# Computing eight experts for all rows, or each for the rows routed to it

## The chip, the cores and the metric

One core of a Trainium2 chip runs the whole program in one launch. The metric is the device time of that core in microseconds, the median of several executions.

## The reference

The input is (16, 512, 192). Two layers run one after the other, each an attention block and a feed-forward block on residuals, after a first block that pools tokens to (16, 128, 192). The block that the change touches is the mixture of experts of the first layer. Rows h2 are the 16 x 128 = 2,048 normalized rows of 192 values:

```python
logits = h2 @ gate_w + gate_b
wts, sel = jax.lax.top_k(logits, TOPK)          # TOPK = 2 of E = 8
wts = jax.nn.softmax(wts.astype(jnp.float32), axis=-1).astype(x.dtype)
cw = (jax.nn.one_hot(sel, E, dtype=x.dtype) * wts[..., None]).sum(axis=1)
res = jnp.zeros_like(h2)
for e in range(E):
    he = jax.nn.gelu(h2 @ w1[e] + b1[e], approximate=False)   # 192 -> 768
    res = res + cw[:, e:e + 1] * (he @ w2[e] + b2[e])         # 768 -> 192
```

Each row has a weight other than zero for two experts only.

## The kernel before

Five engines run instruction lists of their own, written out by hand, with semaphores between them. The order of the stages is: token pooling with attention (`tok_...`, a loop over pairs of batches), two attention stages over 32 units in one schedule (`f_...`, lines 797 to 950 on TensorE), the gate and the experts, an attention with a Sinkhorn iteration (`a_...`, `t_...`), and a quantized feed-forward (`q_...`).

The gate: after `rstd_all("n3")` VectorE normalizes the rows (line 1597), TensorE turns them (line 629), ScalarE writes them out as `feat32` (line 643), and TensorE makes the logits (line 930). VectorE takes the two largest logits with their indices (lines 1601 to 1614) and makes the dense weights `cw`, rows by 8 experts (to line 1630). TensorE turns `cw` (line 938) and multiplies it by the b2 rows (line 943), and VectorE adds that to the residual `hs` (line 1650).

The experts: every product is made of bfloat16 halves, high x high + low x high + high x low. For each of 8 experts and each of 4 groups of 512 rows, `moe_up` (line 657) makes six blocks of 128 hidden values, each of 6 matmuls with 512 columns into one PSUM bank; the weights are the stationary side. ScalarE puts Gelu over each block twice, as bfloat16 (line 1309) and as float32 (line 1312), VectorE subtracts to get the low half (line 1676), and `moe_down` (line 669) multiplies four tiles of 128 rows by 18 matmuls with 192 columns; here the hidden values are the stationary side. VectorE adds each tile, scaled by its column of `cw`, to `hs` (line 1664). All 2,048 rows go through all 8 experts: 128 passes of 128 rows. On TensorE the down blocks of a group stand behind the up blocks of the next. Six experts run in a loop of three turns, two are written out. SyncE loads the weights of two experts ahead (lines 509 to 521), and ScalarE and VectorE split them between groups. GpSimd is idle from line 593 until `moe_done` (line 1686), then clears buffers for the next stage.

## Time and profile before

| | |
|---|---|
| median of 3 executions | 1895.9 us (1895.38 to 1904.0) |
| the profiled execution | 1898.1 us, its span 1896.4 us |
| mean granted TensorE clock | 0.762 of full |
| TensorE busy | 1584.9 us (84%) |
| VectorE busy | 989.3 us (52%) |
| ScalarE busy | 662.5 us (35%) |
| GpSimd busy | 115.6 us (6%) |
| DMA | 25.66 MB, 14 GB/s over the span |

The stages in the span: token stage to about 480 us, attention units to 800, gate to 855, experts to 1302, Sinkhorn attention to about 1765, quantized block to the end. Busy shares are averages over all of them; what a change in one stage is worth is read from that stage. The granted clock is given as a share of 2.4 GHz; it stands at either 1.0 or 0.5 (1.2 GHz) at any moment.

### The profile page before, as it was taken

How to read it: one execution, taken by the hardware profiler on the slowest of the kernel's cores; microseconds unless marked ns; L12 is line 12 of the kernel's file. 1: busy time of each engine (PE TensorE's matmuls, PEld its weight loads, DVE VectorE, ACT ScalarE, POOL GpSimd, SP SyncE). 2: the span in 40 equal slices, each digit the busy share in tenths (PEclk: the TensorE clock that was granted, in tenths of full speed). 3: DMA queues.
4: the chain of work that ended last, by engine and by line, in shares of the span. 5: the costliest groups of instructions: out<-in, count | busy, mean ns of one | idle time of the engine just before them, and what ended most of it. 6: DMA issues, size and time to landing. Idle time of an engine off the chain costs nothing.

```text
span 1896.4 us, 47049 instructions
## 1 busy us (share of the span) xinstructions
PE 1584.9 (84%) x20979; PEld 1301.8 (69%) x20979; DVE 989.3 (52%) x2415; ACT 662.5 (35%) x1116; POOL 115.6 (6%) x90
## 2 busy tenths in 40 slices
PE   6888888888799999879999999997578999996342
PEld 5877778777577777665766676676478898985222
DVE  4445454455356544344444444445446666665777
ACT  1122121222344433137566556653322332213130
POOL 2000000000000000000000000001234222200000
PEclk8767877778799979559999999999655555555566
DMA  4000000020000000000000000000000000000001
GB/s 155 11 7 17 17 17 10 7 66 0 1 2 2 2 2 2 1 25 26 26 16 12 26 26 1 1 1 1 1 3 4 3 4 3 3 3 2 1 1 33
DMA packets 6380, 25.66 MB, mean 14 GB/s; under 512 B 576, under 2 KB 2624, under 8 KB 5952
## 3 DMA queue, kind: packets, MB, share of 16 engines
q1 hardware_dynamic: 6208, 23.05, 3.9%
q8 instruction: 147, 2.41, 0.5%
q14 instruction: 25, 0.20, 0.0%
HBM read 21.47 MB, written 1.57 MB: 12 GB/s over the span
## 4 chain that ended last, share of the span: by engine, by line
PE 68%; DVE 18%; POOL 6%; ACT 6%; issue 2%; POOLq 0%; ACTq 0%; DVEq 0%
PE ps L657 13%; PE ps L669 10%; PE ps L703 6%; PE ps L1031 6%; PE ps L769 4%; PE ps L813 3%; DVE big L430 3%; DVE big L435 3%; POOL big L604 3%; POOL big L608 2%; PE ps L723 2%; PE ps L1079 2%; PE ps L448 2%; PE ps L875 2%; PE ps L838 2%
## 5 line engine op out<-in xcount | busy, mean ns | idle before, releaser
L657 PE MATMUL ps<-big 96*128 96x512 bf16 x1152 | 254.7, 381 | 7.5 <-issue 5.1
L1031 PE MATMUL ps<-big 128*128 128x2 bf16 x7680 | 222.4, 165 | 43.8 <-POOL big L608 20.8
L1031 PEld LDWEIGHTS ps<-big 128*128 128x128 bf16 x7680 | 215.0, 104 | 56.4 <-DVE big L1735 23.8
L1676 DVE TENSOR_TENSOR big<-big 128x512 bf16<-128x512 f32 x192 | 133.0, 693 | 148.9 <-ACT big L1312 148.9
L657 PEld LDWEIGHTS ps<-big 96*128 96x128 bf16 x1152 | 112.6, 98 | 140.4 <-issue 8.3
L669 PEld LDWEIGHTS ps<-big 128*128 128x128 bf16 x2304 | 190.9, 98 | 5.7
L669 PE MATMUL ps<-big 128*128 128x192 bf16 x2304 | 194.1, 246 | 0.0
L1309 ACT ACTIVATE big<-ps,b1cur 128x512 bf16<-128x512 f32 x192 | 131.9, 687 | 161.1 <-PE ps L657 156.1
L448 PE MATMUL ps<-ident,big 128*128 128x128 f32 x384 | 82.6, 397 | 69.3 <-ACT big L442 69.3
L1312 ACT ACTIVATE big<-ps,b1cur 128x512 f32<-128x512 f32 x192 | 130.4, 679 | 0.0
L448 PEld LDWEIGHTS ps<-ident,big 128*128 128x128 f32 x384 | 70.7, 209 | 86.0 <-ACT big L442 86.0
L703 PE MATMUL ps<-consts,big 96*128 96x192 f32 x512 | 114.6, 391 | 12.1 <-POOL iota L593 12.1
L703 PEld LDWEIGHTS ps<-consts,big 96*128 96x128 f32 x512 | 110.8, 260 | 13.0 <-issue 12.0
L1723 DVE TENSOR_REDUCE big<-ps 128x24 f32<-128x48 f32 x160 | 33.0, 206 | 142.2 <-PE ps L1031 141.6
L1664 DVE SCALAR_TENSOR_TENSOR hs<-ps,cwcur,hs 128x192 f32<-128x192 f32 x128 | 51.4, 414 | 81.6 <-PE ps L669 81.6
L442 ACT ACTIVATE big<-big 128x1536 f32<-128x1536 f32 x32 | 47.4, 1483 | 125.2 <-DVE big L435 125.2
L1351 ACT ACTIVATE big<-ps,neg_reg 128x1536 bf16<-128x1536 f32 (+1 forms) x32 | 47.5, 1537 | 108.6 <-PE ps L1016 108.6
L597 POOL MEMSET big<- 128x6144 f32 x1 | 5.2, 5222 | 1290.3 <-DVE small L1686 1290.3
L1541 DVE TENSOR_REDUCE big<-ps 128x12 bf16<-128x1536 f32 x32 | 56.3, 1758 | 50.9 <-PE ps L838 50.9
L1253 ACT ACTIVATE big<-ps 128x512 f32<-128x512 f32 x96 | 50.4, 598 | 89.9 <-PE ps L860 89.9
L430 DVE TENSOR_REDUCE big<-ps 128x3 f32<-128x768 f32 x64 | 58.2, 950 | 43.0 <-PE ps L753 43.0
L769 PEld LDWEIGHTS ps<-big 128*64 128x64 f32 x1536 | 67.8, 185 | 4.3 <-issue 4.3
(314 smaller groups left out, 2440.8 us busy)
## 6 DMA issues: line engine op xcount, KB each, us to landing
big<-w_dram SPq DMA_DIRECT2D x16, 576.0 KB, 5.3
big<-x_dram SPq DMA_DIRECT2D x16, 384.0 KB, 3.4
consts<-packed_dram SPq DMA_DIRECT2D x1, 4459.0 KB, 17.7
out_dram<-hs SPq DMA_DIRECT2D x2, 768.0 KB, 7.0
consts<-packed_dram SPq DMA_DIRECT2D x1, 1152.0 KB, 5.8
```

The source lines that it names most:

```text
L430: last = nc.vector.tensor_reduce(b.mx[:, k * g:(k + 1) * g], sc[:, k], X, ALU.max)
L435: last = nc.vector.tensor_tensor(p4[:, k], sc[:, k], b.mx[:, k * g:(k + 1) * g].unsqueeze(2).to_broadcast([P, g, keys]), ALU.subtract)
L448: last = nc.tensor.transpose(ps[s][:, k // 4, (k % 4) * P:(k % 4 + 1) * P], bufs[s].p[:, k * P:(k + 1) * P], ident[:, :])
L604: nc.gpsimd.affine_select(out=blocks, in_=blocks, compare_op=ALU.not_equal, fill=0.0, base=0, pattern=[[0, HEADS], [-1, P]], channel_multi ...
L657: last = nc.tensor.matmul(ps[0][:, q % 4, :], w1_parts[k][w][:, c, m * P:(m + 1) * P], x[:, c, g * TG:(g + 1) * TG], start=(c == 0 and w = ...
L669: last = nc.tensor.matmul(ps[1][:, t, 0:C], h[g % 2][:, m, t * P:(t + 1) * P], w2_parts[k][w][:, m, :], start=(m == 0 and w == 0 and h is ...
L703: last = nc.tensor.matmul(o[:, t, 0:C], xT[:, c, cols], tok_w[:, c, part * C:(part + 1) * C], start=(c == 0), stop=(c == 1))
L769: last = nc.tensor.matmul(ps[s][w * WQ:(w + 1) * WQ, 3, at:at + HD + 1], pT[:, l, k, w * WQ:(w + 1) * WQ], b.v_ext[:, (2 * w + k) * HEADS ...
L1031: last = nc.tensor.matmul(sums[:, 2 * k:2 * k + 2], kernel_part(i, part)[:, at:at + P], x_parts[g % 4][:, k, 0:2], start=(part == 0), stop ...
L1309: nc.scalar.activation(he_hi[g % 2][:, m, :], ps[0][:, (at - 1) % 4, :], ACT.Gelu, bias=bias)
L1312: nc.scalar.activation(he[:, m, :], ps[0][:, (at - 1) % 4, :], ACT.Gelu, bias=bias).then_inc(sem("moe_gelu"), 1)
L1676: nc.vector.tensor_tensor(he_lo[g % 2][:, m, :], he[:, m, :], he_hi[g % 2][:, m, :], ALU.subtract).then_inc(sem("moe_he_lo"), 1)
```

## The change

The experts are computed on routed rows only. The diff:

- GpSimd prepares counting masks at the start, and SyncE clears a buffer of 39 x 128 rows in DRAM (`xs`). 39 is 4,096 row places in tiles of 128, plus 7 for experts whose last tile isn't full.
- Five experts' weights (7 down to 3) are loaded during the attention stage and split to bfloat16 halves by GpSimd; three (2, 1, 0) by ScalarE and VectorE around the gate. All eight then stay in SBUF (`e_all`). The b1 values become two rows of the contraction, through a small DRAM buffer, so that a hidden block is 5 matmuls.
- TensorE turns `feat32` back to rows (`turn_back`), ScalarE and VectorE split them into a row of 384 bfloat16 values. VectorE and two matmuls count, for each row and choice, its place among its expert's rows, and the expert of each tile (`tile_e`).
- GpSimd sends each row to its two places: 32 indirect DMAs of 128 rows into `xs`. SyncE loads tile after tile, four ahead.
- For each of 39 tiles TensorE reads the expert's number into a register (`value_load`), turns the rows of tile i+2 (`m_turn`, 3 transposes), makes the hidden values of tile i+1 (`m_up`, 30 matmuls with 128 columns; the weights' address comes from the register) and the outputs of tile i (`m_down`, 6 matmuls with 384 columns and 6 with 192). ScalarE makes Gelu twice on 512 and on 256 columns, VectorE copies the rows, subtracts, and sums the two halves of the output. SyncE stores each tile's result to DRAM (`ys`).
- GpSimd fetches the results back by 32 indirect DMAs, and VectorE adds each, scaled by the row's weight, to `hs`. Then `moe_done`.

The core of it:

```diff
-        def moe_up(pe, e, k, g):
-            for m in range(HT):
-                q = g * HT + m
-
-                pe.wait_ge(sem("moe_gelu"), e * (NG * HT) + k * NG * HT + q + 1)
-
-                for c in range(2):
-                    for w, x in ((0, feat_hi), (0, feat_lo), (1, feat_hi)):
-                        last = nc.tensor.matmul(ps[0][:, q % 4, :], w1_parts[k][w][:, c, m * P:(m + 1) * P],
...
+            def m_turn(i):
+                pe.wait_ge(sem(f"m_row{i % 4}"), 16 * (i // 4 + 1))
+                if i >= 2:
+                    pe.wait_ge(sem("m_x"), i - 1)
+                o = ps[1][:, i % 2, 0:ROW // 2].bitcast(BF16)
+                for c in range(3):
+                    last = nc.tensor.transpose(o[:, c * P:(c + 1) * P], e_row[i % 4][:, c * P:(c + 1) * P], identb[:, :])
+                last.then_inc(sem("m_turned"), 1)
+
+            def m_up(i, expert):
+                pe.wait_ge(sem("m_x"), i + 1)
+                if i >= 2:
+                    pe.wait_ge(sem("m_gelu"), 2 * (i - 1))
+                x = e_x[i % 2]
+                sides = (x[:, 0:P], x[:, P:2 * P], x[:, 2 * P:3 * P], x[:, 0:P], e_xe[i % 2])
+                for m in range(HT):
+                    for k, side in enumerate(sides):
+                        at = k * HIDDEN + m * P
+                        w = e_all[:, bass.ds(expert, 1), at:at + P].rearrange("p o n -> p (o n)")
+                        last = nc.tensor.matmul(ps[0][:, 2 * (i % 2) + m // 4, m % 4 * P:(m % 4 + 1) * P], w, side,
+                                                start=(k == 0), stop=(k == CHUNKS - 1))
+                    if m in (3, 5):
+                        last.then_inc(sem("m_up"), 1)
+
+            def m_down(i, expert):
+                if i >= 2:
+                    pe.wait_ge(sem("m_y"), i - 1)
+                o = ps[1][:, 2 + i % 2, 0:2 * C]
+                for m in range(HT):
+                    if m in (0, 4):
+                        pe.wait_ge(sem("m_lo"), 2 * i + 1 + m // 4)
+                    at = CHUNKS * HIDDEN + m * 2 * C
+                    cols = slice(m * P, (m + 1) * P)
+                    for part, n in ((e_hi, 2 * C), (e_lo, C)):
+                        w = e_all[:, bass.ds(expert, 1), at:at + n].rearrange("p o n -> p (o n)")
+                        last = nc.tensor.matmul(o[:, 0:n], part[i % 2][:, cols], w, start=(m == 0 and part is e_hi),
+                                                stop=(m == HT - 1), skip_group_check=True)
+                last.then_inc(sem("m_down"), 1)
...
+            expert = older = None
+            for i in range(-1, TILES):
+                older = expert
+                if i + 1 < TILES:
+                    expert = pe.value_load(tile_e[0:1, i + 1:i + 2], min_val=0, max_val=EXPERTS - 1)
+                if 0 <= i and i + 2 < TILES:
+                    m_turn(i + 2)
+                if i + 1 < TILES:
+                    m_up(i + 1, expert)
+                if 0 <= i:
+                    m_down(i, older)
```

On SyncE (the weight loads and the tiles' rows) and on GpSimd (the split, the sending and the fetching):

```diff
+            sp.wait_ge(sem("m_zero"), 1)
+            sp.dma_start(xs.rearrange("(i p) n -> p i n", p=P),
+                         zero_row.unsqueeze(1).to_broadcast([P, TILES, ROW])).then_inc(sem("m_cleared"), 16)
...
+            sp.wait_ge(sem("m_sent"), 16 * 2 * B)
+            for i in range(4):
+                load_rows(i)
+            for i in range(TILES):
+                sp.wait_ge(sem("m_y"), i + 1)
+                sp.dma_start(ys[i * P:(i + 1) * P, :], e_y[i % 4]).then_inc(sem(f"m_stored{i % 4}"), 16)
+                if i + 4 < TILES:
+                    load_rows(i + 4)
...
+            for n, e in enumerate(EARLY):
+                split_expert(n, e)
+            pool.wait_ge(sem("f_out"), U)
+            for e in LATE:
+                nc.gpsimd.memset(e_up(e, 4), 0.0).then_inc(sem("w_zeros"), 1)
+
+            pool.wait_ge(sem("m_places"), 1)
+            for t in range(B):
+                if t % 2 == 0:
+                    pool.wait_ge(sem("m_rows"), t // 2 + 1)
+                for k in range(2):
+                    nc.gpsimd.indirect_dma_start(
+                        out=xs, out_offset=bass.IndirectOffsetOnAxis(ap=place_i[:, k, t:t + 1], axis=0),
+                        in_=row_parts[:, t, :], in_offset=None).then_inc(sem("m_sent"), 16)
+            for k in range(4):
+                pool.wait_ge(sem(f"m_stored{k}"), 16 * stores(k))
+            for j in range(2 * B):
+                if j >= 8:
+                    pool.wait_ge(sem(f"m_taken{j % 8}"), 16 * (j // 8))
+                nc.gpsimd.indirect_dma_start(
+                    out=taken[j], out_offset=None, in_=ys,
+                    in_offset=bass.IndirectOffsetOnAxis(ap=place_i[:, j % 2, j // 2:j // 2 + 1], axis=0)).then_inc(
+                        sem(f"m_taken{j % 8}"), 16)
```

## Rows read from the trace of the kernel before

**Rows 1.** The page's busy times and its 40 slices, whole span.
```profile
PE 1584.9 (84%) x20979; PEld 1301.8 (69%) x20979; DVE 989.3 (52%) x2415; ACT 662.5 (35%) x1116; POOL 115.6 (6%) x90
...
PEclk8767877778799979559999999999655555555566
```
**Rows 2.** Busy time by stretch: us, each engine, granted clock, DMA share, GB/s.
```profile
500.00:600.00 100.00, 93.22 (x1342) 68.81 (x1341) 51.08 (x136) 41.18 (x88) 0.00 (x0) 1.00 0.01 2
...
660.00:670.00 10.00, 8.52 (x129) 6.71 (x130) 6.88 (x19) 4.48 (x11) 0.00 (x0) 1.00 0.01 2
...
770.00:780.00 10.00, 9.71 (x118) 8.12 (x115) 3.06 (x7) 2.11 (x5) 0.00 (x0) 0.50 0.01 2
...
855.00:1302.00 447.00, 441.36 (x3456) 303.14 (x3456) 204.32 (x342) 268.19 (x412) 0.00 (x0) 1.00 0.05 14
```
**Rows 3.** Instruction groups, 855 to 1302: busy us, mean ns, idle before, releaser.
```profile
L1676 DVE TENSOR_TENSOR big<-big 128x512 bf16<-128x512 f32 x192 | 133.0, 693 | 148.9 <-ACT big L1312 148.9
L1309 ACT ACTIVATE big<-ps,b1cur 128x512 bf16<-128x512 f32 x192 | 131.9, 687 | 161.1 <-PE ps L657 156.1
...
L1664 DVE SCALAR_TENSOR_TENSOR hs<-ps,cwcur,hs 128x192 f32<-128x192 f32 x128 | 51.4, 414 | 81.6 <-PE ps L669 81.6
```
**Rows 4.** The chain that ended last, in order: start us, us, what.
```profile
872.95 5.94 PE ps L669 x72
878.89 7.77 PE ps L657 x36
...
1398.21 14.35 PE ps L1031 x528
```
**Rows 5.** Timeline of the gate and of the end of the experts.
```profile
807.08 5.87 PE L629 MATMUL ps<-ident,big 128*96 128x128 f32 x32 [4.89 <-DVE big L1597]
...
829.48 0.29 DVE L1601 TENSOR_TENSOR logits<-ps,consts 128x128 f32<-128x128 f32 x1 [18.10 <-PE ps L930]
...
833.33 0.18 DVE L1614 CAST gidx<-idx 128x32 f32<-128x32 uint32 x1
...
1302.18 0.06 DVE L1686 MEMSET small<- 128x1 f32 x1
```
**Rows 6.** Instruction groups, whole span: a VectorE copy of 384 columns from PSUM.
```profile
L1452 DVE COPY big<-ps 128x384 f32<-128x384 f32 x16 | 8.9, 558 | 12.5 <-PE ps L736 12.5
```
**Rows 7.** DMAs of lines 504, 521: SyncE's issue in ns; KB and landing in us.
```profile
L504 SPq DMA_DIRECT2D big<-x_dram x14: 317/317/328, 28.8 to 388.7; - x14
...
L521 SPq DMA_DIRECT2D out_dram<-hs x2: 657/674/692, 1887.0 to 1887.8; - x2
...
big<-x_dram SPq DMA_DIRECT2D x16, 384.0 KB, 3.4
```
**Rows 8.** Line 666 on TensorE's sequencer: ns minimum, median, maximum.
```profile
L666 PEldq ALU_OP  x93: 32/32/32, 872.8 to 1188.8; - x93
```
**Rows 9.** Timeline and chain of the first stage: the third load, its first use.
```profile
28.84 2.92 SPq L504 DMA_DIRECT2D big<-x_dram  x2
...
71.28 9.37 PE ps L703 x32
```
**Rows 10.** Timeline of GpSimd, 1504 to 1515 us.
```profile
1504.54 3.29 POOL L608 TENSOR_TENSOR big<-big 128x1536 bf16<-128x1536 f32 x1
...
1511.06 3.10 POOL L608 TENSOR_TENSOR big<-big 128x1536 bf16<-128x1536 f32 x1
```
**Rows 11.** Line 1786 on VectorE, beside GpSimd: ns minimum, median, maximum.
```profile
L1786 DVE TENSOR_TENSOR hs<-hs,big x8: 558/975/1393, 1503.5 to 1764.9; 128x384 f32<-128x384 f32 x8
```
**Rows 12.** The chain from 738 to 790: score blocks of successive units.
```profile
745.84 1.10 PE ps L838 x24
753.49 1.13 PE ps L838 x24
...
772.65 2.05 PE ps L838 x24
782.82 2.05 PE ps L838 x24
```

More of the change, by code:

```diff
@@ new lines, in build, with lists, temp @@
+        lists_at = XQ_AT + 2 * HIDDEN
+        def lists(at, words):
+            return big[:, lists_at + at:lists_at + at + words]
+        below = lists(0, P // 2).bitcast(BF16)
+        ones_b = lists(64, P // 2).bitcast(BF16)
+        ranks = [lists(128 + 96 * k, 96).bitcast(BF16) for k in range(3)]
+        iota_tiles = lists(416, TILES)
+        def temp(at, words):
+            return consts[:, 1920 + at:1920 + at + words]
+        chosen = temp(0, 256).rearrange("p (k b e) -> p k b e", k=2, b=B)
@@ new lines, in _, with row_lo @@
+            nc.vector.tensor_tensor(shifted(ranks[2], 0), shifted(ranks[1], 0), shifted(ranks[1], 64),
+                                    ALU.add).then_inc(sem("m_ranks"), 1)
+            def row_lo(j):
+                dve.wait_ge(sem("m_rows_hi"), j + 1)
+                nc.vector.tensor_tensor(row_parts[:, 2 * j:2 * j + 2, C:ROW], turned_back(j),
+                                        row_parts[:, 2 * j:2 * j + 2, 0:C], ALU.subtract).then_inc(sem("m_rows"), 1)
+            for k in range(4):
+                ins = nc.vector.memset(tile_sums[k], 0.0)
@@ new lines, in _, with sums @@
+            link(ins)
+            for j in range(4):
+                row_lo(j)
+            def sums(k, by=0):
+                return tile_sums[k][:, 4 - by:12 - by]
+            dve.wait_ge(sem("m_ranked"), 1)
+            link(nc.vector.tensor_scalar(sums(0), ps[0][:, 0, 2 * P:2 * P + EXPERTS], 1.0 / P, 0.494, ALU.mult, ALU.add))
+            link(nc.vector.tensor_scalar(sums(0), sums(0), ROUND, ROUND, ALU.add, ALU.subtract))
+            for k in range(3):
+                link(nc.vector.tensor_tensor(sums(k + 1), sums(k), sums(k, 1 << k), ALU.add))
@@ new lines, in _ @@
+            nc.vector.tensor_copy(place_i, place_f).then_inc(sem("m_places"), 1)
+            for j in range(4, 8):
+                row_lo(j)
+            link(nc.vector.tensor_tensor(upto, sums(3).unsqueeze(1).to_broadcast([P, TILES, EXPERTS]),
+                                         iota_tiles.unsqueeze(2).to_broadcast([P, TILES, EXPERTS]), ALU.is_le))
+            link(nc.vector.tensor_reduce(tile_f, upto, X, ALU.add))
+            link(nc.vector.tensor_scalar(tile_f, tile_f, float(EXPERTS - 1), None, ALU.min))
@@ L1683, in _, with m_x @@
-            experts(dve, expert)
-            dve.wait_ge(sem("moe_added"), EXPERTS * B + 4)
+            for k in range(2):
+                nc.vector.memset(e_xe[k][64:P, :], 1.0)
+            late_lo(1)
+            late_lo(2)
+            def m_x(i):
+                dve.wait_ge(sem("m_turned"), i + 1)
+                if i >= 2:
+                    dve.wait_ge(sem("m_up"), 2 * (i - 1))
+                rows = ps[1][:, i % 2, 0:ROW // 2].bitcast(BF16)
+                nc.vector.tensor_copy(e_x[i % 2], rows)
+                nc.vector.tensor_copy(e_xe[i % 2][0:64, :], rows[0:64, P:2 * P]).then_inc(sem("m_x"), 1)
@@ new lines, in _ @@
+            m_x(0)
+            m_x(1)
+            for i in range(-1, TILES):
+                if 0 <= i and i + 2 < TILES:
+                    m_x(i + 2)
+                if 0 < i:
+                    m_y(i - 1)
+                if i + 1 < TILES:
+                    m_lo(i + 1)
+            m_y(TILES - 1)
+            for t in range(B):
+                for k in range(2):
+                    j = 2 * t + k
+                    dve.wait_ge(sem(f"m_taken{j % 8}"), 16 * (j // 8 + 1))
+                    nc.vector.scalar_tensor_tensor(out=hs[:, t, :], in0=taken[j], scalar=gw[:, t, 2 - k:3 - k],
+                                                   in1=hs[:, t, :], op0=ALU.mult, op1=ALU.add).then_inc(sem("m_added"), 1)
+                    dve.wait_ge(sem("m_added"), j + 1)
```

342 lines of the change are left out of this document (215 added, 127 removed).

## The prediction

> **What bounds the kernel now.** I read first the page's busy times and its 40 slices [rows 1], then the engines' busy time by stage [rows 2], then the costliest groups of instructions and the chain of work that ended last, for the expert stage alone [rows 3, 4]. From 855 to 1302 us TensorE is busy 441 of 447 us at a granted clock of 1.00; VectorE is busy 204 and ScalarE 268 [rows 2]. In the chain an up block of 36 matmuls (512 columns each) takes 7.77 us, 215.8 ns apiece, and a down block of 72 (192 columns each) takes 5.94 us, 82.5 ns apiece [rows 4]. Those are 512 and 192 columns at 2.4 GHz plus 2.5 ns: the stage runs at the pace of streamed columns. For one expert and 128 rows this is 36 x 215.8 / 4 + 18 x 82.5 = 3.43 us, and 8 x 16 of them make 439 us, which is the stage. So only fewer columns help, and the change takes a large part of them away: 39 passes of 128 rows in the place of 128. The question is what the routing adds in front of and behind them, where TensorE now has no such wait.
>
> **What goes.** The old path is from the logits, which VectorE takes at 829.48 us, to the small write that releases the next stage, which ends at 1302.24 [rows 5]: 472.8 us.
>
> **What comes, in order of the path.**
>
> *Places.* From the logits to the cast of the indices takes 833.33 + 0.18 - 829.48 = 4.0 us [rows 5], plus nothing new for the gap, which only moves ahead. Behind it stand some 25 small linked VectorE instructions (ranks, tile sums, places) at 0.2 to 0.45 us, about 6 us, and four subtractions of 384 columns out of PSUM at 0.56 each [rows 6]. TensorE's turned-back rows (28 transposes before the rank matmuls) go at the 5.87 us per 32 of the stage before [rows 5] and lie beside it. I take 12.3 us in all.
>
> *Scatter.* 32 indirect DMAs on GpSimd, one behind the other on its queue. The trace has no such instruction. Bounds: SyncE issues a plain DMA of 128 partitions in 0.32 us, and one of 1,024 pieces of 768 bytes in 0.67 us; a plain DMA lands 3.4 us after its issue [rows 7]. A queue is unlikely to beat the first or, as eight may be under way in the gathers, to need the last for each. Software that reads 128 indices and writes 128 addresses is nearest to the 0.67 us of the many-piece row, and slower: I take 1.3 us, twice it. 32 x 1.3 = 41.6 us. The Trainium skill ("DMA: Bandwidth & Descriptors", Latency and other measured facts) gives about 1 us to the first byte of a DMA issued from GpSimd; no row here shows it, and by it, as an estimate, scatter and gather together would take 64 us in the place of 83, and the forecast would be 19 us lower. Under the scatter lie the three late experts' splits (ScalarE about 4.5 us and VectorE about 4 us each), the last of them with a DMA of 5 us or so, the bias rows and the b2 product; should the scatter take under 30 us, these would come forward as the bound and give back up to 10 us.
>
> *Into the loop.* Last landing 3.4, first row tile loaded 3.4 [rows 7], turn and copy 1.4: 8.2 us.
>
> *39 tiles.* TensorE's columns per tile: 30 up matmuls of 128 (55.8 ns each by the 2.5 ns rule above) 1.67 us, 3 turns 0.17, down 6 x (162.5 + 82.5) = 1.47: 3.31 us. That is the lower bound, 129 us. The weight loads don't add to it if they hide as in the old down block, and in the later stage a load and a matmul of two columns go in 14.35 / 528 = 27.2 ns [rows 4], well under 55.8. New is the sequencer's share: each weight address is made in a register. An ALU_OP on TensorE's sequencer takes 32 ns [rows 8]; 30 for the up loads and about 6 for the down ones are 1.15 us, the 90 loads and matmuls at 13.6 ns each are 1.22, five lone waits perhaps 0.25: 2.6 us, under 3.31 and therefore hidden if it can run ahead. Not in the trace is the load of the expert's number into the register, once per tile. Bounds: 0 (hidden behind the queued down matmuls) and 3.4 us (as a DMA's landing), that is a tile of 3.3 to 6.0 us. Small, a read of one word by the sequencer, it is nearer to the lower; I take 1.4 us, a sequencer-bound tile of 4.0 us, 156 us in all. ScalarE needs two activations of 512 at 0.69 and two of 256 at about 0.45, 2.3 us; VectorE 0.56 (x) + 0.25 + 0.69 + 0.43 (low parts) + 0.56 (sum out of PSUM), 2.5 us, with waits 2.8 [rows 3, 6]: neither is the bound. SyncE issues two DMAs a tile (0.7 us) four tiles ahead of need. First tile at the lower clock and the last tile's chain through ScalarE and VectorE: 6 us.
>
> *Here a rule of the skill speaks against the change.* The row shows 192-column pairs at 82.5 ns, loads fully hidden [rows 4]. The Trainium skill ("TensorE: Matmul & The Clock Gate", Back-to-back issue gap) says that streams of load and matmul at 128 columns sustain about 81 ns per matmul, not 56. Were that so, the up part of a tile would be 2.43 us and the tile's columns 4.07, an estimate; it is the first half of rival A below.
>
> *Back.* Last sum and store 4, 32 gathers at 1.3 = 41.6, last landing 3.4 and two additions at 0.42 [rows 3] with their links 0.9: 49.9 us. The additions run behind the gathers, shorter than these.
>
> Sum: 12.3 + 41.6 + 8.2 + 156 + 6 + 49.9 = 274.0 us against 472.8: 198.8 less.
>
> **What is moved elsewhere.** (a) Clearing the row buffer: a store of 3.8 MB is put on SyncE's queue at about 12 us, ahead of the third and fourth input loads. They are issued at 28.8 and first used at 71.3 [rows 9]; even 25 us of store leave 20 us over. If that cover were gone, it would cost what the loads are late, once. (b) Five experts' weights are split on GpSimd during the attention stage, which has no GpSimd work now. A GpSimd subtraction of 1,536 columns takes 3.10 us, and 3.29 beside heavier VectorE work; a VectorE addition of 384 columns that meets it takes 0.56 us at best and 1.39 at worst [rows 10, 11]. So the two disturb each other. GpSimd would need about 12 us per expert, done by about 600 us with loads, long before use. VectorE is busy 51 us in the first 100 us of that stage [rows 2]; 6% of it is 3 us, and one blocked instruction of 0.8 us (384 GpSimd columns) in each of 13 units would be 10. TensorE's chain hides a part; I take 4. (c) The loop's branches and the old memsets go with the old stage, in the 472.8 already. (d) Behind the stage nothing is changed; TensorE arrives cold, but already before it waited 9 us there.
>
> Net: -198.8 + 4 = -194.8. The profiled execution took 1898.1 us (span 1896.4), so 1703 us; the median is 2.2 lower, within the error of all this.
>
> **Rivals.**
> *A. The tile loop is slow* (tile of 5.5 to 6.4 us). Either weight loads, addresses and the register read come one after the other with the matmuls, or TensorE stays at the lower clock: twice 3.2 is 6.4 us. For it: each tile has a sequencer-only instruction between blocks. Against: at 85% busy the attention stage held 1.00 [rows 2]. 39 x (6.4 - 4.0) = +94: 1797 us.
> *B. An indirect DMA takes 2.8 us* on GpSimd: 64 x 1.5 = +96, 1799 us. For it: software per row. Against: nothing in the trace.
> *C. The attention stage loses the clock.* A unit there takes 7.65 us at 1.00 (745.84 to 753.49) and 10.17 at 0.50 (772.65 to 782.82) [rows 2, 12]; it fell by itself late in the stage. If the GpSimd work makes it fall early, up to 24 units x 2.5 us = +61: 1764 us.
> *D. Slower than before.* The indirect DMAs cost over (194.8 / 64) + 1.3 = 4.3 us each, for instance because each waits for its 128 single-row writes in turn (the plain landing of 3.4 us plus 1 us of software). At 5 us the time is 1703 + 64 x 3.7 = 1940 us. It decides from 4.3 us.
> That the change doesn't do what it says is hardly open: 39 tiles are fixed in the code, full or not.
>
> **How the numbers follow.** Forecast 0.62, A 0.14, B 0.14, C 0.06, D 0.04 (of which a quarter within 0.5%). 0.5% is about what a measurement here can tell from no change. The forecast's own lower end has the DMA at 0.67 us (-40) and the tile at 3.3 to 3.6 (-16 to -27): about 1640; its upper end, with 1.8 us and 4.6 us, 1758. To hold 8 in 10 the range takes in most of A and B: 1630 to 1800. Faster 0.95, same 0.01, slower 0.04.
>
> **What would show it.** Right: TensorE idle for about 45 us from 843 us and again for about 48 us before the next stage; between them some 39 equal periods of 4.0 us with the clock at 1.00; GpSimd's queue full in both gaps; the attention stage within 5 us of before. Wrong: periods over 5 us, or at 0.50 (A); gaps over 80 us (B, D); more 0.50 slices before 800 us (C); the first tile waiting for the late weights or bias rows and not for the scatter.

## The result and the profile after

The changed kernel takes 1785.4 us (median of 4 runs, 1782.7 to 1788.4), the kernel before, on the same chip, 1897.0 (4 runs): 0.9405 of it, with an interval of 0.9377 to 0.9434. That is 112 us less; forecast were 195 less, and 1630 to 1800 us as the range. So the direction and the range held, and the forecast's centre was 82 us too low. The profiled execution took 1785.9 us (span 1784.1).

The page of the kernel after, its busy times and the granted clock in 40 slices of 44.6 us (rows 1 of before answer to them):

```profile
PE 1401.8 (79%) x19314; PEld 1182.7 (66%) x19314; DVE 901.0 (51%) x2335; ACT 472.0 (26%) x878; POOL 239.4 (13%) x248
...
PEclk9777786877687978685569999858555555555566
```

TensorE has 183 us less to do. From the twelfth slice on, the attention stage has only one slice at nine tenths, where it had four before [rows 1]. The same as numbers, busy time by stretch (us, each engine, granted clock, DMA share, GB/s); the first three lie in the attention stage, then come the scatter, the loop over the 39 tiles, and the gathers:

```profile
500.00:600.00 100.00, 92.81 (x1130) 67.56 (x1129) 51.86 (x102) 36.22 (x78) 54.40 (x85) 0.86 0.29 86
600.00:700.00 100.00, 92.97 (x1262) 70.21 (x1259) 56.71 (x172) 39.38 (x87) 0.61 (x1) 0.88 0.07 20
700.00:800.00 100.00, 97.15 (x1270) 74.78 (x1268) 40.50 (x91) 33.06 (x74) 0.00 (x0) 0.76 0.01 2
871.00:914.00 43.00, 12.93 (x48) 11.01 (x48) 17.68 (x29) 10.50 (x11) 33.81 (x31) 0.54 0.35 112
918.00:1144.00 226.00, 223.12 (x1755) 160.30 (x1755) 80.30 (x195) 68.00 (x156) 0.00 (x0) 0.98 0.12 35
1147.00:1186.00 39.00, 0.00 (x0) 0.00 (x0) 12.23 (x30) 0.00 (x0) 29.55 (x32) 0.52 0.27 76
```

The marks between the parts, from the timelines of VectorE, GpSimd and TensorE (start us, us, what; in brackets the idle time before and what ended it):

```profile
860.10 0.29 DVE L1781 TENSOR_TENSOR logits<-ps,consts 128x128 f32<-128x128 f32 x1 [17.20 <-PE ps L1042]
...
871.04 1.21 POOL L727 DMA_INDIRECT rows_dram<-consts  x1 [35.01 <-DVE consts L1838]
...
920.14 0.54 PE L1100 MATMUL ps<-big 128*128 128x128 bf16 x3 [0.48 <-DVE big L1891]
...
1143.77 0.56 DVE L1905 TENSOR_REDUCE big<-ps 128x192 f32<-128x384 f32 x1 [0.91 <-PE ps L1116]
1146.82 0.99 POOL L735 DMA_INDIRECT big<-results_dram,consts  x1 [231.50 <-DMA results_dram<-big]
...
1188.92 0.06 DVE L1926 MEMSET small<- 128x1 f32 x1
```

So the logits come 860.10 - 829.48 = 30.6 us later than before [rows 5], although nothing ahead of them was to change but GpSimd's work, the loads of the weights and the clearing of the row buffer. Of these 30.6 us 2.6 lie ahead of the attention stage (its first normalisation starts at 496.76 in the place of 494.19), 28.0 in it. From there the new path takes 1188.98 - 860.10 = 328.9 us, where the old one took 472.8. What follows took 594.2 us before and takes 595.1 now. 30.6 - 143.9 + 0.9 = -112.4, the difference of the spans. Two terms are larger than forecast: the tile loop, and the attention stage.

The loop. The chain of work that ended last, one tile of it, after the same for two more (start us, us, what):

```profile
985.93 1.64 PE ps L1116 x12
987.58 0.17 PE ps L1087 x3
987.74 3.94 PE ps L1100 x30
...
991.68 1.64 PE ps L1116 x12
```

A tile takes 991.68 - 985.93 = 5.75 us at a clock of 1.00. The down block (L1116) takes 1.64 and the turn (L1087) 0.17, near the 1.47 and 0.17 forecast. The up block of 30 matmuls (L1100) takes 3.94, where its columns need 1.67. What TensorE's queue and its sequencer (PEldq) did there, in ns (minimum, median, maximum), and six weight loads in the timeline:

```profile
L1100 PEldq FUSED_REGOPS  x1170: 46/46/65, 920.0 to 1140.3; - x195
L1100 PEld LDWEIGHTS ps<-big x1170: 95/96/105, 920.1 to 1140.4; 128*128 x195
...
L1131 PEldq TENSOR_LOAD <-consts x39: 297/302/491, 919.2 to 1135.8; - x39
...
L1116 PEldq FUSED_REGOPS  x234: 46/46/46, 928.5 to 1142.2; - x117
...
987.92 0.71 PEld L1100 LDWEIGHTS ps<-big 128*128 x6
```

Six loads span 0.71 us and the last lasts 0.096, so they start (0.71 - 0.096) / 5 = 0.123 us apart. Each has a register operation of 46 ns ahead of it, which makes its address. The down block has only 6 of these for its 12 matmuls and longer matmuls to lie behind.

The attention stage. VectorE's normalisation of 192 columns in it (first row before, second row after; SBUF to SBUF), in ns:

```profile
L1531 DVE TENSOR_SCALAR big<-hs,meanvar,rstd x16: 370/374/381, 494.2 to 564.9; 128x192 f32<-128x192 f32 x16
```
```profile
L1711 DVE TENSOR_SCALAR big<-hs,meanvar,rstd x16: 371/379/3726, 496.8 to 575.2; 128x192 f32<-128x192 f32 x16
```

The slowest of 16 took 0.38 us before and 3.73 after. And the score blocks of the units (24 matmuls, 1.10 us at full clock, 2.02 at half): in this stage's chain 5 of 29 were at half clock (granted 0.50, 1.2 GHz) before, and 10 of 29 are after.

The first of the ten, at 564.14 us, comes directly behind this (from the timelines of VectorE and TensorE):

```profile
556.09 2.32 DVE L1703 TENSOR_SCALAR varp<-meanvar 128x4 f32<-128x4 f32 x1
...
561.77 0.66 PE L993 MATMUL ps<-ident,big 128*96 128x128 f32 x2 [3.91 <-DVE big L1728]
```

An instruction of 4 columns took 2.32 us while GpSimd was at work, where its median is 0.17; TensorE, which needs what VectorE makes next, stood idle for 3.91 us, where it had stood 1.09 at this place before; and behind the pause the granted clock is 0.50. GpSimd's last split ends at 600.6 us, so that five of the ten units fall to half clock with GpSimd idle.

### The profile page after: what moved, and what is told of

It reads as the page before. It is cut to its first block, busy times and chain, and to the rows that moved or that the text cites. A ratio compares the mean times of both kernels' runs of the same rounds, so it can differ in the third digit from the quotient of the medians.

```text
span 1784.1 us, 44778 instructions
## 1 busy us (share of the span) xinstructions
PE 1401.8 (79%) x19314; PEld 1182.7 (66%) x19314; DVE 901.0 (51%) x2335; ACT 472.0 (26%) x878; POOL 239.4 (13%) x248
## 4 chain that ended last, share of the span: by engine, by line
PE 61%; DVE 19%; POOL 9%; ACT 6%; issue 3%; DMA 0%; POOLq 0%; ACTq 0%; DVEq 0%
PE ps L1100 8%; PE ps L1212 6%; PE ps L813 6%; PE ps L923 4%; PE ps L879 4%; PE ps L1116 4%; DVE big L497 3%; DVE big L502 3%; POOL big L748 3%; POOL big L752 3%; PE ps L985 2%; PE ps L833 2%; PE ps L948 2%; PE ps L1260 2%; PE ps L515 2%
## 5 line engine op out<-in xcount | busy, mean ns | idle before, releaser
L1212 PEld LDWEIGHTS ps<-big 128*128 128x128 bf16 x7680 | 215.0, 104 | 56.5 <-DVE big L1975 23.9
L1100 PE MATMUL ps<-big 128*128 128x128 bf16 x1170 | 155.8, 229 | 1.1 <-DVE big L1891 0.5
L1100 PEld LDWEIGHTS ps<-big 128*128 x1170 | 111.8, 96 | 42.1 <-issue 3.0
L1898 DVE TENSOR_TENSOR big<-big 128x512 bf16<-128x512 f32 x78 | 43.6, 559 | 116.4 <-ACT big L1494 114.2
L1493 ACT ACTIVATE big<-ps 128x512 bf16<-128x512 f32 x78 | 38.2, 490 | 178.8 <-issue 140.9
L748 POOL TENSOR_SCALAR_AFFINE_SELECT big<-big 128x1536 f32<-128x1536 f32 (+1 forms) x32 | 48.8, 1550 | 244.3 <-ACT big L1531 244.3
L1531 ACT ACTIVATE big<-ps,neg_reg 128x1536 bf16<-128x1536 f32 (+1 forms) x32 | 47.5, 1536 | 108.3 <-PE ps L1197 108.2
L696 POOL MEMSET big<- 128x768 bf16 x5 | 3.7, 738 | 531.7 <-DMA consts<-w_dram 531.7
L923 PE MATMUL ps<-big,consts 96*96 96x512 f32 (+1 forms) x128 | 74.2, 713 | 0.6 <-ACT big L1411 0.3
L879 PE MATMUL ps<-big 128*64 128x17 f32 x1536 | 69.8, 245 | 0.0
L1545 ACT ACTIVATE big<-big 128x128 f32<-128x128 f32 x192 | 56.9, 386 | 37.2 <-DVE big L2004 37.2
```

Of the source, the lines that this page charges most:

```text
L748: nc.gpsimd.affine_select(out=blocks, in_=blocks, compare_op=ALU.not_equal, fill=0.0, base=0, pattern=[[0, HEADS], [-1, P]], channel_multi ...
L879: last = nc.tensor.matmul(ps[s][w * WQ:(w + 1) * WQ, 3, at:at + HD + 1], pT[:, l, k, w * WQ:(w + 1) * WQ], b.v_ext[:, (2 * w + k) * HEADS ...
L923: last = nc.tensor.matmul(f_qk_bank(g), w[rows, c, part * C + co * HC:part * C + (co + 1) * HC], f_xT[block % 2][rows, c, :], start=(c == ...
L1100: last = nc.tensor.matmul(ps[0][:, 2 * (i % 2) + m // 4, m % 4 * P:(m % 4 + 1) * P], w, side, start=(k == 0), stop=(k == CHUNKS - 1))
L1212: last = nc.tensor.matmul(sums[:, 2 * k:2 * k + 2], kernel_part(i, part)[:, at:at + P], x_parts[g % 4][:, k, 0:2], start=(part == 0), stop ...
L1545: last = nc.scalar.activation(block, block, ACT.Exp, scale=l1_sv[:, at:at + 1])
```

## The experiments

Twelve kernels; in seven of them part of the work is left out or changed, as each expectation says. Two kernels can differ by 10 us or more through the attention stage alone, whose length varies, between kernels and between executions of one kernel (experiment 4); so the stages of the profiles are compared as well as the medians. "The loop" is counted from the first turn to the start of the last sum, 918.7 to 1143.8 or 225.1 us in the changed kernel.

**1. Are the register addresses the cost?** The expert of each tile fixed at build time:

```
-                    expert = pe.value_load(tile_e[0:1, i + 1:i + 2], min_val=0, max_val=EXPERTS - 1)
+                    expert = (i + 1) * EXPERTS // TILES
...
-                        w = e_all[:, bass.ds(expert, 1), at:at + P].rearrange("p o n -> p (o n)")
+                        w = e_all[:, expert, at:at + P]
```

> The changed kernel with the expert of each of the 39 tiles fixed when the kernel is built (tile i takes expert 8i/39): no number is read into a register and no weight address is made in one; all else stays. It leaves out the choice of the expert by the data, so rows meet the wrong weights. Theory 1 (TensorE's sequencer sets the tile: each of 30 up weight addresses costs it 46 ns, some 49 ns more until the weight load starts, and the load waits in line): the up matmuls come 56 to 60 ns apart, an up block takes about 1.8 us in the place of 3.94, the tile 3.3 to 3.6 us in the place of 5.74, the whole 1690 to 1700 us. Theory 2 (a load and a matmul of 128 columns can't follow each other faster than 81 ns, the Trainium skill's figure): up block 2.4 us, tile 4.1, whole about 1720 us. Theory 3 (ScalarE or VectorE or the row DMAs set the tile): it stays at 5.7 us and 1785.

1715.2 us (1703.1 to 1718.8), 0.9024 of before. By the median alone that is nearest to theory 2 (1720), but in the timeline the 30 up matmuls take 1.67 us before the down block starts, which only theory 1 allows. And with the number still read but not used:

> The same fixed experts (so rows meet the wrong weights here too), but the expert's number is still read into TensorE's register once per tile, with its range assertion, and then not used. If the read lies behind the queued down matmuls, as the trace of after suggests, this is within 0.1 us per tile (4 us in all) of the kernel with no read. If the read of 0.30 us and its 0.2 us of register work are on the path, it is 12 to 20 us slower than that.

1692.2 us (1687.5 to 1707.2). This one had a shorter attention stage (logits at 834.9 us, against 859.0 in the other); the loops take 155.6 (fixed) and 152.4 us (fixed, number read), in the place of 225.1. So reading the number costs nothing that can be seen, and the addresses cost 70 to 73 us as long as the next bound stands behind them. But the tile did not reach 3.3 us. The chain of the kernel that still reads the number:

```profile
986.57 0.35 PE ps L1087 x3
...
987.22 0.20 DVE big L1892
987.43 0.47 DVE big L1906
987.92 0.32 SPq L616
...
988.28 1.95 DMA big<-rows_dram
...
990.28 0.35 PE ps L1087 x3
```

A ring of 990.28 - 986.57 = 3.71 us: turn, copy of x, then the sum of an earlier tile behind it on VectorE, SyncE's store and load, the row load's landing, the next turn. The sum of tile i is taken when tile i + 1 is under way, and SyncE issues the load of row tile i + 4 only behind it, by which time TensorE is about to ask for it. Theory 3 had named the row DMAs, but as what holds the tile at 5.7 us; that they come next, at 3.7, none of the theories had.

**2. The ring taken away.** The load is issued ahead of the wait for the sum:

```
             for i in range(TILES):
+                if i + 4 < TILES:
+                    load_rows(i + 4)
                 sp.wait_ge(sem("m_y"), i + 1)
                 sp.dma_start(ys[i * P:(i + 1) * P, :], e_y[i % 4]).then_inc(sem(f"m_stored{i % 4}"), 16)
-                if i + 4 < TILES:
-                    load_rows(i + 4)
```

> The kernel with fixed experts and the number still read (rows meet the wrong weights), and with one more edit: SyncE issues the row load of tile i+4 before it waits for the sum of tile i, and not behind that wait. With fixed addresses the trace shows a ring of 3.76 us per tile: sum (0.48), its issue on SyncE (0.32), row load (2.0 to 2.6), turn (0.35), copy of x (0.45). If that ring is what holds the tile there, it now falls to TensorE's columns, 3.3 to 3.5 us, and the whole to 1672 to 1682 us. If 3.76 is what TensorE can do with 128-column matmuls (the Trainium skill's 81 ns would ask for 4.07), it stays at 3.7 or above.

1688.4 us (1666.7 to 1696.3), with a late attention stage (logits at 856.3) in the profile; the loop takes 131.6 us, 93.5 less than in the changed kernel. Its chain, and the loads (ns):

```profile
982.03 0.17 PE ps L1087 x3
982.20 1.68 PE ps L1100 x30
983.87 1.47 PE ps L1116 x12
...
985.51 1.68 PE ps L1100 x30
...
L1100 PEld LDWEIGHTS ps<-big x1170: 97/98/152, 916.2 to 1043.1; 128*128 128x128 bf16 x195
```

A tile takes 985.51 - 982.20 = 3.31 us, to the digit the 3.31 forecast from columns, and 30 matmuls 1.68 (forecast 1.67). So streams of a load and a matmul of 128 columns go at 56 ns here, once their addresses are fixed. The Trainium skill ("TensorE: Matmul & The Clock Gate", Back-to-back issue gap) gives about 81 ns for them; this run disagrees.

**3. A third of the addresses, with registers.** The rows become the loaded operand, the weights stream, 5 matmuls of 512 and 5 of 256 columns (the row loads ahead as in experiment 2; the loops around these lines are left out here):

```
-                        last = nc.tensor.matmul(ps[0][:, 2 * (i % 2) + m // 4, m % 4 * P:(m % 4 + 1) * P], w, side,
+                        last = nc.tensor.matmul(ps[0][:, 2 * (i % 2) + half, 0:n], side, w,
```

> The changed kernel with its register-made addresses, but the up products with the roles exchanged: the rows are the loaded operand (fixed address) and the weights stream, 5 matmuls of 512 columns and 5 of 256 per tile in the place of 30 of 128. The columns are as many as before (3,840), the addresses a third. The row loads go ahead of the sum's wait as in the kernel beside it. It leaves out turning the hidden values back, so the down products meet them the wrong way round. If each address costs the sequencer some 124 ns in line (46 for making it, 49 until the operand is taken, the rest for issue), the up part falls from 3.94 to 1.6 or 1.7 us, the tile to 3.3 to 3.6 and the whole to 1690 to 1705 us. If instead a register-addressed operand is slow to stream or the reading of the number is the cost, the tile stays over 5 us.

1678.7 us (1656.6 to 1693.2), 0.8863 of before, below the 1690 to 1705 expected; the logits come at 827.3 us in its profile, and its loop takes 129.8. Its up block and its register operations:

```profile
L1100 PEldq FUSED_REGOPS  x390: 46/46/65, 887.0 to 1010.2; - x195
...
984.75 1.62 PE ps L1100 x10
986.38 1.47 PE ps L1115 x12
```

As many columns, the same 46 ns for each address, but 10 addresses in the place of 30: 1.62 us in the place of 3.94. Streaming from an address in a register is not slow, then. What costs is one address per short matmul: the sequencer needs 123 ns for such a pair, the array 56. That settles what holds the loop of the changed kernel. One thing stays open: the addresses are now those of streamed operands, and before they were those of loaded ones, so no run tells how far the 123 ns go with an address as such or with its being that of a loaded operand.

**4. GpSimd in the attention stage.** First the splits of the five early experts left out:

```
-            for n, e in enumerate(EARLY):
-                split_expert(n, e)
             pool.wait_ge(sem("f_out"), U)
+            for e in EARLY:
+                nc.gpsimd.memset(e_all[:, e, :], 0.0).then_inc(sem("w_early"), 7)
...
```

> The changed kernel without GpSimd's splitting of the five early experts during the attention stage; their loads stay, and their weights are set to zero by GpSimd behind that stage. It leaves out five experts' weights. If GpSimd's work is what made the attention stage 28 us longer (it blocks VectorE, and TensorE's clock falls early), the logits come at 830 to 838 us in the place of 860 and the whole takes 1755 to 1765 us. If the loads do it, or if the clock just falls where it likes, the logits stay at 850 to 865 and the whole at about 1785. If only GpSimd's blocking of VectorE counts and not the clock, 3 to 10 us are gained.

1777.2 us (1769.3 to 1778.5), between what the theories gave: 1755 to 1765 for GpSimd's work as the cause, 1785 for chance. In its attention stage 5 units are at half clock, as before, and the last score block starts at 784.4 us (782.8 before, 814.1 in the changed kernel); but the logits come at 852.8. The profile says why. GpSimd's memsets, put behind the stage, met VectorE's statistics (timeline, start us and us):

```profile
804.29 5.22 POOL L718 MEMSET big<- 128x6144 bf16 x1 [790.83 <-DVE big L1738]
805.90 3.63 DVE L1675 TENSOR_SCALAR varp<-meanvar 128x16 f32<-128x16 f32 x1
...
809.57 5.27 DVE L464 TENSOR_SCALAR rstd<-varp 128x16 int32<-128x16 int32 x1
809.60 5.21 POOL L718 MEMSET big<- 128x6144 bf16 x1
```

An instruction of 16 columns on VectorE took 5.27 us, the length of the memset that it met, and 3.63 us, to the end of the one before (804.29 + 5.22 = 809.51 and 805.90 + 3.63 = 809.53). The experiment had moved its own disturbance to a worse place. With the weights zeroed by DMA:

```
+            for e in EARLY:
+                sp.dma_start(e_all[:, e, :], xs[0:16 * P, :].rearrange("(p i) n -> p (i n)", i=16)).then_inc(
+                    sem("w_early"), 16)
```

> The changed kernel without GpSimd's splits of the five early experts, and with their weights zeroed by DMA (7.9 MB from DRAM between 500 and 600 us) and no longer by GpSimd, whose setting to zero held up VectorE in the earlier kernel of this kind. It leaves out five experts' weights. If the GpSimd work costs the attention stage its 29 us, the logits come at 826 to 834 us in the place of 860, and the whole takes 1750 to 1762. If DMA traffic in that stage costs something too, it shows here, with more traffic than the changed kernel has: later than 840. If it was chance, 1780 to 1790.

1750.7 us (1748.7 to 1753.1), 0.9235 of before, where the changed kernel has 0.9405: (0.9405 - 0.9235) x 1897 = 32 us less. Logits come at 823.4 us, with 4 units of 29 at half clock. The stretches that answer to the first two above:

```profile
500.00:600.00 100.00, 93.21 (x1361) 68.19 (x1360) 50.78 (x136) 42.81 (x91) 0.23 (x5) 1.00 0.51 169
600.00:700.00 100.00, 92.49 (x1259) 69.91 (x1257) 54.39 (x165) 39.81 (x87) 0.00 (x0) 0.88 0.01 2
```

At 169 GB/s of DMA the stage keeps 1.00 in its first 100 us: traffic is not the cause. From the other side, the splits alone in the kernel before:

> The kernel before, with the GpSimd work of the five splits alone put into its attention stage (same operations, sizes and number, on scratch memory, from the first normalised tile on; no loads). If that work is the cause of the longer stage, the time rises by 20 to 30 us, to 1915 to 1925, with slices of TensorE's clock below 1.00 between 500 and 650 us. If the loads are the cause or chance, it stays within 5 us of before.

1943.9 us (1924.5 to 1955.4), 1.0206 of before, interval 1.0146 to 1.0266: 39 us slower by the ratio and 45 by the medians, more than expected (the profiled execution, the fastest, took 1924.5), with 9 of 29 units at half clock and

```profile
500.00:600.00 100.00, 96.50 (x885) 68.55 (x886) 34.14 (x75) 29.77 (x63) 52.42 (x81) 0.67 0.01 1
```

So GpSimd's work alone does it. Here it runs without pause, and from 497 us on, on the stage's first normalisations.

How sure are the 30 us? Eight of the kernels profiled here share the changed kernel's splits and everything ahead of the logits. From the first normalisation to the logits they take 363.3 us (the changed kernel, 10 units at half clock), 363.5 (10) and 340.9 (5) in experiment 1, 364.5 (10) and 340.7 (6) in experiments 2 and 3, 369.4 (11) in experiment 5, and 343.8 (7) and 340.6 (5) in the two whole versions with splits of experiment 6. Without the splits it is 335.3 (5) in the kernel before and 331.7 (4) in the one whose weights are zeroed by DMA. So in these profiles the splits cost 5 to 34 us against the kernel before, and the changed kernel's 28.0 are at the long end. In all eight, TensorE's pause at the place shown above is 2.3 to 4.8 us and the very next unit is the first at half clock, between 554 and 565 us; in the three kernels whose GpSimd is idle there (these two and the one with memsets behind the stage) the pause is 1.09 and the first such unit comes at 678 to 683.

The same kernel varies as well: executions of one are up to 37 us apart with the splits (1656.6 to 1693.2 in experiment 3, 1755.6 to 1787.5 in experiment 5, though only 1782.7 to 1788.4 in the changed kernel), and 4 apart in the kernel zeroed by DMA. So what is shown is that the splits hold up VectorE, that the first fall of the clock follows the pause which this makes, and that the same work alone makes the kernel before slower. How many units fall later, with GpSimd idle, varies; what decides it stays open. In the kernel before a fall comes at 681 us, behind a pause of only 1.2.

**5. The indirect DMAs on GpSimd.** Half of the rows, here in the scatter, and likewise in the rows sent and in the gathers:

```
-                        out=xs, out_offset=bass.IndirectOffsetOnAxis(ap=place_i[:, k, t:t + 1], axis=0),
+                        out=xs, out_offset=bass.IndirectOffsetOnAxis(ap=place_i[0:64, k, t:t + 1], axis=0),
```

> The changed kernel with each of the 64 indirect DMAs on GpSimd cut to the first 64 of its 128 rows. It leaves out half of the routed rows. In the changed kernel one takes 0.96 us of GpSimd and 0.30 us pass until the next. If the 0.96 us are spent per row, one now takes about 0.5 us and the pace is 0.8: 64 x 0.46 = 29 us less, about 1756 us (the scatter may then wait for other work and give back up to 10 of it). If they are a fixed cost of the instruction, nothing changes: 1780 to 1790.

1776.0 us (1755.6 to 1787.5), 0.9318 of before (0.9264 to 0.9372): 16 us less than the changed kernel by the ratios, between the two theories (29 less, or nothing). The runs are 32 us apart, and the profile is of the longest, so the stages decide. Scatter and gathers take 41.8 and 38.2 us in the place of 44.3 and 39.8, together 4 less, where the theory of a cost per row asked for 29. The rest isn't seen in this profile. First the scatter's row of the changed kernel (128 rows each; ns), then scatter and gather with 64:

```profile
L727 POOL DMA_INDIRECT rows_dram<-consts x32: 959/963/2982, 871.0 to 914.4; - x32
```
```profile
L727 POOL DMA_INDIRECT rows_dram<-consts x32: 887/892/1843, 876.2 to 917.1; - x32
L735 POOL DMA_INDIRECT big<-results_dram,consts x32: 888/895/917, 1149.7 to 1187.0; - x32
```

963 against 892 ns: as an estimate from these two, 1.1 ns per row and 0.82 us fixed. The cost is the instruction's, for the most part, and not the rows'.

**6. Whole versions.** The wide up block needs the hidden values turned back: 12 more transposes on TensorE and a copy each on ScalarE and VectorE.

```
+                    for m in range(HT):
+                        cols = slice(m * P, (m + 1) * P)
+                        last = nc.tensor.transpose(dst[:, cols], src[i % 2][:, cols], identb[:, :])
```

> A whole version: up products with streaming weights (10 register addresses in the place of 30), rows loaded ahead, and the hidden values turned back by 12 more transposes of 128 columns on TensorE, with one more copy of 768 columns each on ScalarE and VectorE. Columns per tile: 3.31 + 12 x 0.0558 = 3.98 us; VectorE 2.8 + 0.8 = 3.6; ScalarE 2.3 + 0.9 = 3.2. By the theory of the sequencer the tile takes 4.0 to 4.4 us and the whole 1715 to 1735 us. If the longer chain through ScalarE and VectorE isn't covered by the extra stage in the pipeline, 4.5 to 5 us and up to 1760. If register addresses aren't the cause, 1785 and above.

1709.8 us (1695.7 to 1728.2), 0.8999 of before (0.8925 to 0.9074), a little under the 1715 to 1735 expected; its loop takes 164.1 us, 4.2 per tile. Then the splits taken off GpSimd as well (high parts to ScalarE), with the low parts on VectorE or left on GpSimd:

> The whole version with streaming up weights, and two more edits. The splits of the five early experts leave GpSimd: ScalarE makes the high parts (9 copies of 384 columns per expert, three behind each of three units), VectorE the low parts (7 subtractions, two or three behind each of three units), 45 x 0.4 = 18 us on ScalarE and 35 x 0.45 = 16 us on VectorE within 240 us in which they are busy 42% and 50%. And SyncE issues the row loads one tile further ahead. If GpSimd's hold on VectorE was what cost the attention stage up to 30 us, the logits come at 825 to 840 us, and the loop goes at 3.98 us per tile: 1680 to 1700 us for the whole. If any work added to VectorE and ScalarE there delays the units as much and lets the clock fall, the logits stay at 845 to 862 and the whole at 1700 to 1725.

> The same, but the low parts are made by GpSimd: its 35 subtractions of 384 columns stay (some 28 us of its 57), only its copies go to ScalarE. If each GpSimd instruction holds up VectorE's SBUF work, about half of the loss stays: the logits at 830 to 855 us, the whole 5 to 15 us behind the version that uses VectorE. If it is VectorE's own time that is scarce, this one is the faster by as much.

1749.2 us (7 runs, 1719.8 to 1751.8), 0.9216 of before, and 1749.9 us (5 runs, 1743.2 to 1750.4), 0.9206: both about 40 us worse than the version that they start from, and the first is 24 us over the highest value expected. Nor is the second 5 to 15 us behind the first. From the first normalisation to the logits they take 365.0 and 395.6 us, with 8 and 14 units at half clock; the first profile is of its fastest execution, 29 us under its median. In both the edit also put five short memsets on GpSimd at the very start of the stage, and they met the first normalisations; five of these take 3.65 us in the first of the two kernels:

```profile
497.14 3.88 POOL L755 MEMSET big<- 128x768 bf16 x5 [483.69 <-DVE big L1772]
...
497.84 3.65 DVE L1772 TENSOR_SCALAR big<-hs,meanvar,rstd 128x192 f32<-128x192 f32 x5 [0.53 <-PE ps L948]
...
524.08 2.02 PE ps L986 x24
537.52 2.01 PE ps L986 x24
```

and the second and third unit run at half clock, as they do in the kernel before with splits (523.6 and 537.0 us), whose GpSimd work also begins at 497 us. The eight kernels whose GpSimd work begins behind the first weight load, 9.6 to 11.6 us after the first normalisation (at 507 us in the changed kernel) and not 0.5, had these units at full clock. So part of the loss of these two is probably that start, and how much the moved splits themselves cost stays open. It wasn't tried without the memsets.

Last, the first whole version with the row loads one tile further ahead:

```
+            load_rows(4)
             for i in range(TILES):
-                if i + 4 < TILES:
-                    load_rows(i + 4)
+                if i + 5 < TILES:
+                    load_rows(i + 5)
```

> The whole version with streaming up weights and GpSimd's splits as in the changed kernel, and with the row loads issued one tile further ahead: in that version one of the row loads in the middle of the loop took 3.3 us and was on the path. If these loads are what keeps its loop at 164 us where TensorE's columns ask for 39 x 3.98 = 155, the loop now takes 156 to 159 us and the median falls by 5 to 8 us, to 1700 to 1706 (with a spread of 15 us either way from the clock of the attention stage, which this edit doesn't touch). If they aren't, 1710.

1702.5 us (6 runs, 1685.9 to 1717.1), 0.8993 of before, interval 0.8960 to 0.9027: (0.9405 - 0.8993) x 1897 = 78 us less than the changed kernel. Its loop takes 157.8 us, that of the first whole version 164.1, where five row loads of 2.7 to 3.5 us stand in the chain between 960 and 1045 us; here none does. That the loop is 6 us shorter is thus shown by the profiles, but not by the whole time: 0.8993 and 0.8999 can't be told apart. Its chain:

```profile
985.25 1.57 PE ps L1111 x9
986.83 0.67 PE ps L1122 x12
987.50 1.47 PE ps L1136 x12
988.97 0.17 PE ps L1098 x3
989.13 1.62 PE ps L1111 x10
```

1.62 up, 0.67 to turn back, 1.47 down and 0.17 to turn the rows: 3.93 us per tile. These two are the fastest whole kernels of this study.

## Why the prediction was right or wrong

*What bounds, and what goes.* Right. The expert stage was bound by columns, and with 39 passes in the place of 128 the 472.8 us of the old path are gone as counted. That the measured time lies within the range, 15 us under its upper end, is owed to the range's having been widened for rivals A and B; the sum itself was 82 us off, by two terms that both came out too small.

*Places.* 12.3 us forecast; 871.04 - 860.10 = 10.9 measured. Right within its error.

*Scatter.* 41.6 forecast at 1.3 us each; 871.0 to about 915.3, 44.3 us. One takes 0.96 us and 0.30 pass until the next, and a few take longer. The guess, twice the row of many pieces, came out right by luck, since its reason (work per row) was wrong: by the estimate of experiment 5, 0.82 of 0.96 us don't depend on the rows. The Trainium skill's figure for a first byte ("DMA: Bandwidth & Descriptors", Latency and other measured facts) would have made it 1.0 us each; the pace is 1.27. Rivals B and D (2.8 and over 4.3 us each) are out.

*Into the loop.* 8.2 forecast, 915.3 to 920.1 is 4.8. The two landings were taken from a 384 KB load; the row loads of this kernel are a quarter as large (96 KB) and land in a median of 2.0 us.

*39 tiles.* This step failed, in the term of the sequencer. Columns per tile: 3.31 us forecast, 3.31 measured as soon as addresses are fixed and rows come early (experiment 2). Register read: taken at 1.4 us on the path, found at nothing. The addresses: the sum was 36 x 32 ns for making them and 90 x 13.6 ns for issue, with waits 2.6 us in all, below the columns and so hidden. Measured: the register operation takes 46 ns and not 32, and load and matmul don't follow it at 13.6 ns each: a pair with an address comes each 123 ns. The 13.6 came from a stage whose addresses are fixed [rows 4], and was carried to instructions that wait for a register. 30 x 0.123 = 3.7 us for the up block alone, above its columns. The value taken, 4.0 us per tile, was thus a sum of a cost that isn't there (1.4) and one sized at less than half. With 6 us for the ends 162 us were forecast, and 920.1 to 1144.3 is 224.2: 62 us. Rival A named this mechanism ("weight loads, addresses and register read come one after the other"), at 5.5 to 6.4 us; the tile took 5.75. It got 0.14, and from its own argument it should have had more: the only evidence against it concerned the clock, the other half of that rival, and that stayed at 1.00.

*SyncE four tiles ahead.* Wrong, though it cost nothing in the changed kernel: the load waits behind the sum, a ring of 3.7 us that the slow up block hid (experiment 1). It would have been the bound in the forecast's own lower case of 3.3 us.

*Back.* 49.9 forecast; 1144.3 to 1189.0 is 44.7. The gathers pace at 1.25 us as the scatter does.

*Splits in the attention stage.* This step failed too: +4 us forecast, +28.0 in this profile, 32 by the ratios with and without them (experiment 4), and 5 at least in every profile with them. The direct hold was sized well: the sum counted one VectorE instruction held up by 0.8 us in each of 13 units, 10 us, and VectorE's SBUF to SBUF instructions with a scalar took about 12 us longer in this stage. What was wrong is the step from 10 to 4, that TensorE's chain hides a part. The chain adds to it instead: the hold can last for several of GpSimd's instructions in a row (2.32 us, where 0.17 was usual), TensorE pauses, and behind the pause the granted clock is at 0.50 for more units, at 14.7 us from one to the next in place of 8 to 9. Rows 11 had shown 0.56 to 1.39 us, and that was taken for the size of a meeting. Rival C (up to +61, chance 0.06) was this mechanism, and it was half true: fewer units than its 24 fell, and each cost more than the 2.5 us which it had taken from the late units [rows 12].

*Clearing the row buffer.* Right: the logits' delay has no part of it, since the first unit starts at 512.85 us against 510.29, and that whole stage differs by 2.6 us. (Other kernels of this study with the same instructions up to there start that unit at 502.7 to 512.0, so the 2.6 us say little.)

Sum of the misses: 62 in the loop, 27 in and ahead of the attention stage, 1 behind, less 7 for the four parts that came out shorter or longer in small ways (-1.4 + 2.7 - 3.4 - 5.2 = -7.3). That is 83, where 82 are to be explained. Rivals A and C came true together, in part each, where each had been given a chance as if alone.

## What to carry to other kernels

- A loaded operand whose address is made in a register puts a serial stretch on TensorE's sequencer for each instruction: compare it (0.12 us here) with what the array needs for that instruction. Give such addresses to few, long matmuls, by exchanging the operands if need be, and let the short ones have fixed addresses. A longer route on the array (12 more transposes per tile) paid for it here.
- An engine that is idle in a stage is not free if it shares memory with one that paces the stage. Look at where its instructions would meet the other's short SBUF work, above all at the start of a stage, and don't count on a TensorE-bound stage to hide a delay: here the clock added to it.
- When a bound falls, look for the ring behind it: a transfer issued behind a wait for the previous result is early only as long as something else is late.

## What the runs showed of the hardware that was not expected

- A pair of weight load and 128-column matmul: 56 ns with fixed addresses, 123 ns with the loaded operand's address made in a register ahead of each. The reading of a word into the register takes 0.30 us of the sequencer and was hidden behind queued matmuls.
- A GpSimd memset of 6,144 bf16 columns took 5.2 us, and a VectorE instruction of 16 columns that met it 5.27 us: it waited the whole of it out. VectorE's reductions and copies out of PSUM kept their times beside GpSimd's work (1.758 us for a reduction of 1,536 columns and 0.36 for a copy of 192, before and after).
- The Trainium skill ("SBUF — State Buffer", Who interferes with whom) says that a VectorE instruction in a mode that takes the pair of ports it shares with GpSimd, such as a tensor_scalar from SBUF to SBUF, and a GpSimd one block each other for the whole instruction, and that reductions never do. The rows agree: 5.27 us for a tensor_scalar beside a memset of 5.21, and 1.758 us unchanged for the reduction.
- An indirect DMA on GpSimd: 0.96 us with 128 rows and 0.89 with 64, 0.30 us apart.
- The same instructions from the first normalisation to the logits took 341 to 369 us in eight profiles, with 5 to 11 units at half clock; the first fall came in each directly behind a pause of TensorE of 2.3 to 4.8 us.
- The instructions ahead of that stage took 486.6 to 496.8 us in the same eight.
